# Fused decoder, first stage: weight quantisation split in two steps with ScalarE's help, context clipping on ScalarE, taps and inverse transform moved

## The reference

```python
# layer 0, attention: autocorrelation per row, 6 best lags, softmax-weighted sum of rolled rows
f = rfft(x); corr = irfft(f * conj(f)); w, delay = top_k(corr, 6)
x = x + sum(roll(x, delay_k) * softmax(w)_k)
# layer 0, cross attention: both operands fake-quantised to 0..255
q = clip(round(v / s + z), 0, 255);  x = x + (q1 - z) s1 @ (q2 - z) s2
# layer 0, ffn: weights in MX form, a power-of-two scale for every 32 elements
scale = 2 ** (floor(log2(amax)) - 2)
step  = 2 ** max(floor(log2(|w / scale|)), 0) / 2          # fp4, 1 mantissa bit
wq    = clip(round(w / scale / step) * step, -6, 6) * scale
```

## Time and profile before

| | us |
|---|---|
| median of 3 runs | 1315.38 (1312.62 to 1319.81) |
| the profiled execution, as timed | 1316.73 |
| its span, first to last instruction | 1314.9 |
| PE busy / mean granted clock over the span | 1154.2 / 0.938 |
| DVE busy | 898.0 |
| ACT busy | 547.8 |
| POOL busy | 538.3 |

### The profile page before, as it was taken

The page is one execution under the profiler, slowest core; times in us unless marked ns, Lnnn a source line. Parts: engine busy times, 40 slices in busy tenths (PEclk is TensorE's granted clock), DMA queues, the critical chain, the costliest instruction groups (busy, mean ns, idle before and its releaser), DMA issues.

```text
span 1314.9 us, 16908 instructions
## 1 busy us (share of the span) xinstructions
PE 1154.2 (88%) x5655; PEld 886.9 (67%) x5660; DVE 898.0 (68%) x1432; ACT 547.8 (42%) x1094; POOL 538.3 (41%) x372
## 2 busy tenths in 40 slices
PE   4929723759899999999999999879999999997999
PEld 2413311327588888888888888755788888875887
DVE  6999998896586877777777777655454545543543
ACT  1211322312565656565656565632453535342011
POOL 3774430010465555555555555510454544441000
PEclk9968955888999999999999999989999999998899
DMA  7172442101101010101111000240001010011121
GB/s 296 65 237 95 144 161 91 32 32 33 46 23 53 25 52 24 44 32 33 43 24 52 22 30 13 79 146 24 7 15 35 12 30 0 1 37 52 64 90 70
DMA packets 38834, 77.70 MB, mean 59 GB/s; under 512 B 11395, under 2 KB 19588, under 8 KB 35588
## 3 DMA queue, kind: packets, MB, share of 16 engines
q1 hardware_dynamic: 37188, 71.86, 16.5%
q0 software_dynamic: 1600, 5.24, 1.3%
HBM read 69.75 MB, written 9.44 MB: 60 GB/s over the span
## 4 chain that ended last, share of the span: by engine, by line
PE 76%; DVE 14%; issue 4%; ACT 4%; POOL 1%; DMA 1%; SPq 1%; POOLq 0%; DVEq 0%; ACTq 0%
PE PS L1439 17%; PE PS L1441 17%; PE PS L1440 17%; PE PS L1513 9%; PE PS L1479 6%; PE PS L1356 2%; PE PS L1407 1%; PE PS L1610 1%; PE PS L1307 1%; PE PS L1304 1%; ACT arena L739 1%; DVE blkamax L916 1%; DMA cs<-in_freqs 1%; PE PS L1579 1%; PE PS L1288 1%
## 5 line engine op out<-in xcount | busy, mean ns | idle before, releaser
L555 POOL TENSOR_TENSOR arena<-arena,rsum 128x768 f32<-128x768 f32 x192 | 281.7, 1468 | 440.9 <-DVE rsum L1119 440.9
L1114 DVE TENSOR_REDUCE nmax<-PS 128x1 f32<-128x768 f32 x192 | 183.1, 954 | 150.0 <-PE PS L1441 148.8
L739 ACT ACTIVATE arena<-PS,nmax 128x768 f32<-128x768 f32 x192 | 173.4, 903 | 25.8 <-DVE nmax L1114 25.5
L755 ACT ACTIVATE PTH<-PS 128x384 fp32r<-128x384 f32 x256 | 111.9, 489 | 166.5 <-PE PS L1513 166.4
L1513 PE MATMUL PS<-identf,arena 128*128 128x128 f32 x1152 | 158.0, 273 | 2.3 <-DVE PTL L1162 0.9
L1513 PEld LDWEIGHTS PS<-identf,arena 128*128 128x128 f32 x1152 | 129.9, 140 | 4.8 <-POOL arena L555 3.5
L1162 DVE TENSOR_TENSOR PTL<-PS,PTH 128x384 fp32r<-128x384 f32 x256 | 129.6, 547 | 2.3 <-ACT PTH L755 1.5
L1119 DVE RECIPROCAL rsum<-psum_exp 128x1 f32<-128x1 f32 x192 | 31.5, 164 | 88.9 <-ACT arena L739 83.8
L1479 PE MATMUL PS<-arena 128*96 128x256 f32 x384 | 87.6, 379 | 2.5 <-ACT arena L761 1.0
L761 ACT ACTIVATE arena<-PS 128x384 f32<-128x384 f32 x64 | 31.4, 490 | 127.4 <-PE PS L1513 127.4
L542 POOL TENSOR_TENSOR WQL<-arena,WQH 128x512 fp32r<-128x512 f32 (+1 forms) x48 | 58.3, 1218 | 61.0 <-ACT WQH L615 61.0
(11 more groups left out here) (243 smaller groups left out, 2555.8 us busy)
## 6 DMA issues: line engine op xcount, KB each, us to landing
arena<-in_wq SPq DMA_DIRECT2D x32, 256.0 KB, 2.6
arena<-in_wo SPq DMA_DIRECT2D x8, 1024.0 KB, 4.8
arena<-in_expert_w SPq DMA_DIRECT2D x8, 1024.0 KB, 4.8
arena<-in_wgu SPq DMA_DIRECT2D x11, 512.0 KB
arena<-v_dram SPq DMA_DIRECT2D x8, 384.0 KB, 3.5
arena<-in_wq SPq DMA_DIRECT2D x16, 192.0 KB, 2.9
arena<-in_wo SPq DMA_DIRECT2D x4, 768.0 KB, 5.3
arena<-in_wd SPq DMA_DIRECT2D x4, 704.0 KB
```

The costliest lines, as they stand in the source:

```text
L555: pool.tensor_tensor(PR[:, u % 4, :], PR[:, u % 4, :], rsum[:, u % 4:u % 4 + 1].broadcast_to([P, KEYS]), ALU.mult).then_inc(s["pn_ready"], 1)
L739: act.activation(PR[:, slot, :], SC[pair][:, 0:KEYS], ACT.Exp, bias=nmax[:, slot:slot + 1], accum_out=psum_exp[:, slot:slot + 1]).then_inc ...
L755: act.activation(fr(PTH[:, (u // 4) % 2, 3 * half:3 * half + 3, u % 4 * P:(u % 4 + 1) * P]), bank(B_PT[half])[:, 0:3 * P].rearrange("p (k ...
L1114: dve.tensor_reduce(nmax[:, slot:slot + 1], SC[pair][:, 0:KEYS], AX.X, ALU.max, negate=True)\
```

## The change

A chunk is now quantised in two DVE functions. `weight_normalised(c)` makes the scales, normalises and takes the exponent. `weight_rounded(c)` adds and subtracts the magic number and clips. Between the two ACT makes the magic number (`magic(c)`, an activation with a bias operand, bf16 out). DVE does `weight_normalised(c + 1)` ahead of `weight_rounded(c)`. POOL multiplies by the scale for every chunk (`scaled`) and normalises none. Both uses of the magic number are now one `scalar_tensor_tensor`, which adds `ROUND / 2` to ACT's output and subtracts.

The context's clipping leaves POOL: after POOL's first scaling, three chained activations on ACT clip and round it (`context_clipped`), and POOL finishes with one instruction that takes its two scalars from a tensor. POOL gathers the taps four at a time between the `scaled` of chunks 3 to 7 (before, all 20 in a row). PE runs the inverse transform ahead of chunk 1's transposes (before, behind). `CONTEXT_AT` moves steps 2 to 7 a chunk later, and `TAPS_AT` the taps from chunks 5, 6, 8, 9 to chunks 9, 10, 11, 12. Two small tensors (6 words for every partition) are added ahead of the large arena.

```diff
-        SHARED = 6
-        CONTEXT_AT = {0: (0, 1), 1: (2, 3), 2: (4, 5), 3: (6, 7), 5: (8, 9), 6: (10, 11), 7: (12, 13), 8: (14, 15)}
-        TAPS_AT = {5: 0, 6: 1, 8: 2, 9: 3}
+        CONTEXT_AT = {0: (0, 1), 2: (2, 3), 3: (4, 5), 4: (6, 7), 5: (8, 9), 6: (10, 11), 7: (12, 13), 8: (14, 15)}
+        TAPS_AT = {9: 0, 10: 1, 11: 2, 12: 3}
...
# SP
-            load_chunk(5)
+            for c in range(5, 8):
+                load_chunk(c)
             sp.wait_ge(s["ectx_psum"], 8)
             sp.dma_start(CTXT, ctx_t[1].rearrange("(k p) t -> p k t", p=P)).then_inc(s["ctxt_in"], 16)
-            for c in range(6, len(CHUNKS)):
+            for c in range(8, len(CHUNKS)):
                 load_chunk(c)
...
# POOL
+            def context_quantised(n):
                 pool.wait_ge(s["ctxn_in"], 16 * (n + 1))
                 pool.tensor_scalar(CN, CN, inv_s[:, 1:2], qs[:, 3:4], ALU.mult, ALU.add)\
-                    .then_inc(s["pool_chain"], 1)
-                pool.wait_ge(s["pool_chain"], 2 + 2 * n + 1)
-                pool.tensor_scalar(CN, CN, 0.0, 255.0, ALU.max, ALU.min).then_inc(s["pool_chain"], 1)
-                pool.wait_ge(s["pool_chain"], 2 + 2 * n + 2)
-                pool.tensor_scalar(CQ[:, n // 2, (n % 2) * 2:(n % 2) * 2 + 2, :], CN, ROUND, -(ROUND + 128.0),
-                                   ALU.add, ALU.add).then_inc(s["cn_used"], 1)
+                    .then_inc(s["cn_scaled"], 1)
+                pool.wait_ge(s["cn_clipped"], n + 1)
+                pool.tensor_scalar(CQ[:, n // 2, (n % 2) * 2:(n % 2) * 2 + 2, :], CN, qconst[:, 0:1], qconst[:, 1:2],
+                                   ALU.mult, ALU.add).then_inc(s["cn_used"], 1)
...
+            context_quantised(0)
+            context_quantised(1)
+            for c in range(3):
                 scaled(c)
+                if c < 2:
+                    context_quantised(c + 2)
+            pool.wait_ge(s["h2_out"], 32)
+            pool.wait_ge(s["off_ready"], 1)
+            for c in range(3, len(CHUNKS)):
+                for n in range(4 * (c - 3), min(4 * (c - 2), RT * LAGS)):
+                    gather(n)
+                scaled(c)
...
# ACT
+            def magic(c):
+                act.wait_ge(s["wexp_ready"], c + 1)
+                if c >= 2:
+                    act.wait_ge(s["wq_rounded"], c - 1)
+                act.activation(weight_magic(c), WM[:, 0:CHUNKS[c]], ACT.Relu, bias=neg_magic[:, 0:1],
+                               scale=ROUND / 2).then_inc(s["magic_ready"], 1)
...
+            def context_clipped(n):
+                act.wait_ge(s["cn_scaled"], n + 1)
+                act.activation(CN, CN, ACT.Identity, bias=qconst[:, 2:3]).then_inc(s["act_chain"], 1)
+                act.wait_ge(s["act_chain"], 2 * n + 1)
+                act.activation(CN, CN, ACT.Relu, bias=qconst[:, 3:4], scale=-1.0).then_inc(s["act_chain"], 1)
+                act.wait_ge(s["act_chain"], 2 * n + 2)
+                act.activation(CN, CN, ACT.Relu, bias=qconst[:, 4:5], scale=-1.0).then_inc(s["cn_clipped"], 1)
...
+            for c in range(len(CHUNKS)):
+                if c + 2 < len(CHUNKS) and c != 2:
+                    magic(c + 2)
+                for w in [c] if c < NCH else [2 * c - NCH, 2 * c - NCH + 1]:
+                    weight_step(w)
+                for n in CONTEXT_AT.get(c, ()):
+                    context_step(n)
+                if c < 2:
+                    context_clipped(c + 2)
+                if c + 1 in TAPS_AT:
+                    tap_diagonals(TAPS_AT[c + 1])
+                if c == 2:
                     act.wait_ge(s["tap_diff"], 1)
                     act.activation(tapw[:], tapv[:], ACT.Exp).then_inc(s["tap_exp"], 1)
+                    magic(c + 2)
...
# DVE
+            def weight_normalised(c):
+                n = CHUNKS[c]
+                w, nn = WX[:, c % 2, 0:n], weight_normal(c)
                 dve.wait_ge(s[f"wx_in{c % 2}"], 16 * (c // 2 + 1))
+                if c >= 3:
+                    dve.wait_ge(s["wq8_ready"], c - 2)
+                block_scale(w, n, 0.25, blkinvs[c % 3], blkscales[c % 3])
+                dve.tensor_tensor(blocks(nn, n), blocks(w, n), spread(blkinvs[c % 3], n // MX), ALU.mult)\
+                   .then_inc(s["wx_used"], 1)
+                dve.wait_ge(s["wx_used"], c + 1)
+                if c:
+                    dve.wait_ge(s["magic_ready"], c)
+                dve.tensor_scalar(WM[:, 0:n].bitcast(U32), nn.bitcast(U32), EXPONENT, None, ALU.bitwise_and)\
+                   .then_inc(s["wexp_ready"], 1)
+
+            def weight_rounded(c):
+                n = CHUNKS[c]
+                nn, mm, q = weight_normal(c), weight_magic(c), WQ8[:, c % 2, 0:n]
+                dve.wait_ge(s["magic_ready"], c + 1)
+                step(dve.scalar_tensor_tensor(nn, mm, ROUND / 2, nn, ALU.add, ALU.subtract))
                 if c >= 2:
                     dve.wait_ge(s["wt_psum"], c - 1 if c - 2 < NCH else NCH + 2 * (c - 2 - NCH) + 2)
-                step(dve.tensor_tensor(q, nn, mm, ALU.subtract))
-                step(dve.tensor_scalar(q, q, 6.0, -6.0, ALU.min, ALU.max))
-                dve.tensor_tensor(blocks(q, n), blocks(q, n), spread(blkscale, nb), ALU.mult)\
-                   .then_inc(s["wq8_ready"], 1)
...
+                step(dve.scalar_tensor_tensor(q, mm, ROUND / 2, nn, ALU.add, ALU.subtract))
                 dve.tensor_scalar(q, q, 6.0, -6.0, ALU.min, ALU.max).then_inc(s["wq_rounded"], 1)
```

More of the change, by code:

```diff
@@ L482, in _ @@
             pool.memset(minus_half[:], -0.5).then_inc(s["consts"], 1)
+            pool.memset(neg_magic[:], -ROUND / 2).then_inc(s["consts"], 1)
+            for i, v in enumerate((1.0, -128.0, ROUND, ROUND + 255.0, 255.0)):
+                pool.memset(qconst[:, i:i + 1], v).then_inc(s["consts"], 1)
             pool.wait_ge(s["pool_chain"], 2)
@@ L515, in gather @@
                     .then_inc(tap_in[r], 16)
-            def normalised(c):
-                n, nb = CHUNKS[c], CHUNKS[c] // MX
-                pool.wait_ge(s["scales_ready"], c - SHARED + 1)
-                pool.tensor_tensor(blocks((WN, WN2)[c % 2][:, 0:n], n), blocks(WX[:, c % 2, 0:n], n),
-                                   spread(blkinvs[c % 3], nb), ALU.mult).then_inc(s["wn_ready"], 1)
             def scaled(c):
@@ L657, in _ @@
                 act.activation(SQ[:, m, :], bank(m), ACT.Square).then_inc(s["sq_ready"], 1)
-            for w in range(NCH + 2 * (D // P)):
-                if w == 3:
+            for c in range(len(CHUNKS)):
[10 more added lines that the diff above has]
+                if c == 2:
                     act.wait_ge(s["tap_diff"], 1)
                     act.activation(tapw[:], tapv[:], ACT.Exp).then_inc(s["tap_exp"], 1)
-                weight_step(w)
-                if w in TAPS_AT:
-                    tap_diagonals(TAPS_AT[w])
-                for n in CONTEXT_AT.get(w, ()):
-                    context_step(n)
+                    magic(c + 2)
             squared(1)
@@ L930, in weight_chunk @@
                 dve.wait_ge(s[f"wx_in{c % 2}"], 16 * (c // 2 + 1))
-                block_scale(w, n, 0.25)
-                chain[0] += 1
-                dve.tensor_tensor(blocks(nn, n), blocks(w, n), spread(blkinv, nb), ALU.mult)\
-                   .then_inc(s["dve_chain"], 1)
-                dve.wait_ge(s["dve_chain"], chain[0])
-                step(dve.tensor_scalar(mm.bitcast(U32), nn.bitcast(U32), EXPONENT, None, ALU.bitwise_and))
-                dve.sem_inc(s["wx_used"], 1)
-                step(dve.tensor_scalar(mm, mm, 1.0, ROUND / 2, ALU.max, ALU.mult))
@@ L940, in weight_chunk @@
-                step(dve.tensor_tensor(nn, nn, mm, ALU.add))
+                if c >= 3:
[6 more added lines that the diff above has]
+                    dve.wait_ge(s["magic_ready"], c)
@@ L956, in chunk_rounded @@
-            def chunk_rounded(c):
-                n = CHUNKS[c]
-                nn, mm, q = (WN, WN2)[c % 2][:, 0:n], WM[:, 0:n], WQ8[:, c % 2, 0:n]
-                dve.wait_ge(s["wn_ready"], c - SHARED + 1)
-                step(dve.tensor_scalar(mm.bitcast(U32), nn.bitcast(U32), EXPONENT, None, ALU.bitwise_and))
-                step(dve.tensor_scalar(mm, mm, 1.0, ROUND / 2, ALU.max, ALU.mult))
-                step(dve.tensor_tensor(nn, nn, mm, ALU.add))
-                dve.wait_ge(s["wt_psum"], c - 1 if c - 2 < NCH else NCH + 2 * (c - 2 - NCH) + 2)
-                step(dve.tensor_tensor(q, nn, mm, ALU.subtract))
+                step(dve.scalar_tensor_tensor(q, mm, ROUND / 2, nn, ALU.add, ALU.subtract))
@@ L993, in _ @@
             step(dve.tensor_copy(iota8[:], iota8i[:]))
-            weight_chunk(0)
-            weight_chunk(1)
+            weight_normalised(0)
+            weight_normalised(1)
+            weight_rounded(0)
+            weight_normalised(2)
+            weight_rounded(1)
             dve.wait_ge(s["sq_ready"], KT)
@@ L999, in _ @@
```

(19 more changed lines are left out.)

56 lines of the change are left out of this document (23 added, 33 removed).

## The result

| | before | after |
|---|---|---|
| median of the runs made together, us | 1315.08 | 1301.78 |
| lowest to highest, 4 runs each | 1312.62 to 1319.81 | 1299.66 to 1303.25 |
| profiled execution, as timed / span | 1316.73 / 1314.9 | 1303.25 / 1301.4 |
| the edited stage ends (layer norm starts) at | 186.26 | 173.85 |
| from there to the end | 1128.6 | 1127.6 |

The ratio is 0.9896, with a 95% interval of 0.9878 to 0.9914: 13.7 us less, against the 14.2 of the sum. Of the 13.5 us by which the profiled spans differ, 12.4 arise before the layer norm (0.8 of them ahead of DVE's first chunk, which began at 22.42 us and no longer at 23.25), and 1.1 in the unedited rest.

What follows compares the result with a forecast made beforehand. DVE's row of instructions was taken to bound the edited stage. 77.5 + 0.5 + 87.6 + 4 + 2.5 = 172.1 against 186.3 gave 14.2 us less, hence 1301 us; forecast 1293 to 1308, range 1290 to 1310.

Steps and rivals of the forecast that it cites:

- the sum: Whole edited stage: 77.5 + 0.5 + 87.6 + 4 + 2.5 = 172.1 us against 186.3, 14.2 us less.
- The first part: Stage up to the lag weights' exponential: DVE waits 6 to 10 us for ACT and goes on at 77.5.
- The chain: Context loads, POOL scaling, ACT clipping, PE steps and ACT copies in series ahead of the exponential, which ends at 77.5 us.
- The second part: DVE from the lag weights on: normalising chunks 5 to 14, rounding 4 to 14, 87.6 us, plus one stall of 4.
- The stall for chunk 8: Near 101 us DVE waits 4 us for a chunk load queued behind the second half of the transposed context.
- The port: SBUF ports shared by DVE and POOL: nothing counted for DVE's two-SBUF-input additions and subtractions waiting on POOL's multiply.
- The 9.5 us that I had worked out from the rule: Chunks 3 to 7: up to 1.9 us each if DVE's additions and subtractions waited for POOL's late multiply; not counted.
- Rival (c): DVE's 30 new combined instructions are slow: 1328 us at double length, deciding from 1.5 times a `tensor_tensor`; chance 0.05.
- What I called hidden: Magic numbers on ACT (1.1 and 1.5 us), gathers in fours, inverse transform and taps: claimed to cost DVE no time.
- (a): Before the exponential and at the chunk load, ACT in time or loads fast: 1289 us without all waits; chance 0.08.
- (b): The context's chain or PE is slower, by POOL's last step or PE's low clock: 1309 us; chance 0.12.
- (d): Behind the stage, key cache loads wait for the last taps, the gain is lost and nothing changes; chance 0.01.

Runs made afterwards that it cites:

- e5b: Changed kernel with the context's clipping and rounding back on POOL as two instructions with immediates, ACT's clipping activations gone; 1299.47 us, ratio 0.9862.
- e6b: Changed kernel with chunk 14's two combined instructions made plain subtractions without the added constant, so its weights differ from the reference; one execution, 1303.18 us.
- e3: Changed kernel with DVE's four tap sums ahead of chunk 14's rounding instead of behind it; ratio 0.9886 to the kernel before.
- e8b: Changed kernel with all 20 gathers in a row on POOL ahead of chunk 3's multiply; 1312.28 us, ratio 0.9956.
- e7b: Changed kernel with the taps back behind chunks 5, 6, 8 and 9, diagonals still made one chunk ahead; 1309.23 us, ratio 0.9933.
- e1: Changed kernel with the lag weights' exponential ahead of chunk 2's copy on ACT and chunk 4's magic number behind that copy; 1293.49 us, ratio 0.9825.

## Why the prediction was right, point by point

**The total.** 1301 us was forecast and 1301.78 measured, by the steps' own mechanism: DVE sets the end of the stage, with two waits. That the total is so close is in part luck. The stage gained 12.4 us and not 14.2; the unedited rest, for which the sum had nothing, gave 1.1, which is within what it moves by itself. Inside the stage the parts erred both ways by up to 3.3 us.

**The first part** ended at 79.45, not 77.5. The chain, as forecast and as it ran (end of each, us):

| | forecast | after |
|---|---|---|
| POOL has scaled piece 1 | 32.9 | 33.2 |
| ACT has clipped it | 36.5 | 36.7 |
| `scaled(0)` | 39.7 | 41.3 |
| PE's context steps 0, 1 | 48.1 to 49 | 51.5 |
| POOL has finished piece 2 | 53.9 | 56.9 |
| piece 3 scaled | 59.8 | 61.6 |
| `scaled(2)` | 66.6 | 68.3 |
| context steps 2, 3 | 76.7 | 78.7 |

(From 39.7 the working's own terms, 0.8 and 7.06, give 47.6, not 48.1; the 49 that it went on with covers the slip.) Two terms were too small and one too large. POOL's L513, L516 and L530 took 1.85, 2.17 and 2.34 us for piece 1, where 1.20, 1.20 and 1.91 are usual, about 2 more in all; in each case one of DVE's large instructions was running when they began. The pairs of context steps took this in PE's timeline:

```profile
42.15 9.38 PE L1323 MATMUL PS<-arena 128*96 128x512 f32 x16
...
69.14 9.53 PE L1323 MATMUL PS<-arena 128*96 128x512 f32 x16
```

against 7.06 in the earlier trace rows; I had allowed 1 and 2 us more, and it was 2.3 and 2.5. The granted clock was 0.73 from 41.3 to 51.6 us and 0.72 from 68.3 to 78.7, after idle times of PE of 4.1 and 8.9 us; before, it was 1.00 from 37.0 to 44.7, where the 7.06 stands. The load of piece 3 took 3.5 us instead of the 4.7 of the estimate. L516 was 1.20 where it ran alone, so the choice of L502's operations as its like, over L507 at 3.96, held. DVE itself came later than I reckoned: it was through with its own work at 73.54, not between 67.6 and 71.6, so it waited 5.9 us and not 6 to 10.

**The second part**, from the exponential to the tap sums, took 91.9 us against 92.1. The stall for chunk 8 was 4.87 (4 forecast): the transposed context was issued at 97.55 instead of 95, the chunk was there 9.4 us later instead of 10.9, and DVE wanted it at 102.1 instead of 101. The normalisings and roundings took 3.3 less than the sum. I charged chunks 11 and 12 for a multiply of 1408 columns while POOL was still at ones of 1024, 1.2 us together; the roundings of 1024 columns took 2.86 and not 2.98, 0.8 over seven; and the five normalisings to which I gave 0.7 for POOL's multiply took 1.1 less, L954 being delayed by 0.62 on the mean. And 2.2 us came at chunk 14, of which the sum had none. The last taps ended on PE at 166.1 (152 reckoned), 5 us ahead of the tap sums; PE had idled 3.7 us ahead of the last group, for POOL's multiply, so it had no work waiting, and it is not the bound.

**The port.** This is the step that failed: "I count nothing for it". The row under it, L940 beside L507, was no test, because L507 is one of POOL's long instructions, with immediate operands. e5b shows the two kinds: L980 at 54.53 ran at its usual 1.23 us inside L518 (52.06 to 56.02), and at 42.87, beside the multiply L532, it took 2.81. POOL's instructions with immediate operands are not free either: L977 at 52.45 took 2.04 us beside L518, where 1.22 is usual, and in the trace of before, which I had, DVE's small L919 took 0.99 and 1.04 us beside L505, where 0.18 is usual.

The rule of the Trainium skill ("SBUF — State Buffer", "SBUF: two separate sides"), a lock for a whole instruction and against two SBUF inputs too, agrees with L982 (3.86 against 1.62), with e6b (3.87) and with e3, where additions with one source in PSUM went free. It does not agree with POOL's long instructions with immediates, beside which a DVE instruction with two SBUF sources was held for 0.8 us at most.

What the sum missed by it is more than the 2.2 us at chunk 14. POOL's three instructions for piece 1, on the chain to the exponential, lost about 2 us (POOL's rows, then DVE's):

```profile
36.79 2.17 POOL L516 TENSOR_SCALAR arena<-arena,qconst 128x1024 bf16<-128x1024 f32 x1 [3.64 <-ACT arena L677]
38.92 2.34 POOL L530 TENSOR_TENSOR arena<-arena,blkscale 128x1024 bf16<-128x1024 bf16 x1
```

```profile
39.42 2.92 DVE L979 SCALAR_TENSOR_TENSOR arena<-arena 128x1024 f32<-128x1024 bf16 x1
```

And DVE's instructions in the first part that took longer than their usual length, this one among them, add up to 7.5 us. These were taken out of DVE's wait for the exponential and cost nothing. The 9.5 us that I had worked out from the rule did not come, because POOL's multiplies of chunks 3 to 7 began when DVE was at its maximum or waiting.

**The new instruction** costs what a `tensor_tensor` costs: 1.22 to 1.23 and 1.62. Rival (c) is dead in its cause as well. The rule of the Trainium skill on half speed ("Vector Engine (DVE) Microarchitecture Reference", "Points that are easy to get wrong") is not touched by it, since one source here is bf16.

**What I called hidden.** The magic numbers (1.14 and 1.47 us) were: no wait of DVE names them. The gathers in fours were, and e8b shows that a row of 20 is not. The taps are the weak point: I wrote that they have slack at their new place, which held, but not that their old place would have cost; by e7b their move is worth 9.3 us of the stage and about 5 in the timed runs. The clipping on ACT, which the steps costed with care, is worth nothing by e5b.

**The other rivals.** (a), ACT in time, was ruled out for this order, and e1 makes it true with two moved instructions: 1293.49 us by its own measurement, 0.7% below the changed kernel; rival (a) said 1289 for both waits gone. (b) happened in small: PE's two pairs took 1.8 us more than I had allowed. (d) did not: the rest is 1127.6 against 1128.6 us.

## What to carry to other kernels

Where an engine's order is written by hand, ask of each small instruction that another engine waits for what stands ahead of it that it does not need: one exponential behind unrelated copies made waits of 9.9 us, 5.9 directly and 4 through the loads that hang on it, and the stage was 8.4 us shorter without them. Put POOL's multiplies so that they meet reductions or PSUM sources on DVE, and mind the last round of a pipeline, where the work that covered it is missing. A row that is to rule out a contention must have the same kind of instruction on both sides.
